# Resident feedforward weights: split in the cross attention before it, or tile by tile in the first batch that uses them

## The chip, the cores and the metric

One core of a Trainium2 chip runs the whole program. The metric is the device time of one execution in microseconds (us). TensorE does the matrix products, VectorE and ScalarE the elementwise work, GpSimd some elementwise work, and SyncE (SP) issues most of the transfers.

## What is computed

Six layers in a row over 2048 tokens of 512 features (8 batches of 256): a quantised attention, a cross attention, a feedforward with experts, an attention, a long convolution and a ternary feedforward. Each adds to its input and is followed by a layer norm. The change touches the second and the third:

```python
scores = einsum('bsd,bmd->bsm', x, ctx) / sqrt(512)          # cross attention
attn = softmax(where(mask, scores, -1e30)); out = einsum('bsm,bmd->bsd', attn, ctx)

gate_base, up_base = xf @ Wg.T, xf @ Wu.T                    # feedforward, DFF = 1408
base_out = silu(gate_base) * up_base @ Wd.T
topw, topi = top_k(softmax(xf @ Wr.T), 2)                    # 2 of 8 experts, rank 16
h = silu(gate_base + 2 * xf @ Ag.T @ Bg.T) * (up_base + 2 * xf @ Au.T @ Bu.T)
out = base_out + sum(we * 2 * h @ Ad.T @ Bd.T)
```

## The kernel before

Every layer is a stage of its own, with a barrier between stages. In a stage each engine has a list of work written out by hand; engines wait for each other on semaphores and run their lists strictly in order.

Large products are done with each operand split in two: a high part (the value copied to the rounded type fp32r, by ScalarE or VectorE) and a low part (the value minus its high part). A product is three matmuls: high by high, low by high, high by low.

**Cross attention** (`cross_attention`, L766) goes over 16 tiles of 128 tokens, two to a batch. In a step s TensorE turns tile s (L899), makes the scores of tile s-1 (L908), the output of tile s-3 (L917) and turns the probabilities of tile s-2 (L926). ScalarE copies what was turned (L938, L952) and takes the exponential (L945); VectorE masks the scores (L987 to L990), adds the output to x (L1001) and normalises. SP loads x and the context of a batch into one of three slots (L846 to L850); batch b waits until both tiles of batch b-3 are added (`added`).

In the same steps the stage prepares the feedforward's resident weights, in tiles that outlive it (`keep["experts"]`). They come as 20 pieces: AgT and AuT, AdT in two parts, WgT and WuT in halves of each of their four row blocks, of 256 to 384 KB, through five slots of `c_raw`. SP issues five pieces behind the loads of three batches, later ones as slots become free (`w_low`). ScalarE makes the high part (L957, after its copies of the step) and VectorE the low part (L1017, last in the step), one or two pieces a step.

**The feedforward** (`expert_feedforward`, L1024) has 8 batches of FT = 11 tiles of 128 hidden features; a step t is such a tile (NS = 88). `base(t)` is 24 matmuls, xhi and xlo by wg and wu (L1201). `expand` adds an expert's low rank part on top (L1214), choice 1 one step and choice 2 two steps later. `down` multiplies by ad (L1227) and wd (L1238). TensorE's order in a step t is: expand(t-2, 2), expand(t-1, 1), base(t), then some preparation of the next batch (turn x, logits, turn masks, `low_rank`, a "misc" item each, in one shared PSUM bank that the reader frees with `misc_read`), and down(t-1). Before the loop stand the preparation of batch 0 and base(0) to base(2).

ScalarE's order in a step is: the silu of choices 2 and 1 (L1335), items of the preparation, the silu of choice 0, the high part of the hidden values (L1381), and `weights_high(t+1)`: wait for entry t+1, high part of wd (L1343) and of bg (L1347). In step 5 `powers` takes an exponential (L1308), which costs a change of ScalarE's table and another back. VectorE's order is: `hidden_low` and `down_low` of the step before, the hidden values of choices 2 and 1 (L1463), `expand_low(t)` (L1482), parts of the routing (steps 4 to 8), and the hidden values of choice 0.

Streamed weights come in **entries**: entry e is Bg and Bu of tile e and WdT of tile e-1 (L1108 to L1110), in two slots. SP may issue entry e when entry e-2 is split (`entry_split`, raised by expand_low(e-2)). x comes in three slots of `xt`, loaded by ScalarE's queue (L1285).

Of the kernel before, what the change touches and what calls it, by code (L numbers as in the profile page):

```python
# [22 lines left out]
P = 128  # L23
# [742 lines left out]
def cross_attention(nc, io, sem, keep):  # L766

    NT = N // P
    XT, CT, RAW, HALF = 6, 3, 5, DFF // 2
    CUT = ((0, 6), (6, FT))
    ER = E_ * R_
    BLOCKED = 1e30
    held = ExitStack()
    fix = Maker(nc, held)
    keep["experts"] = own = dict(
        held=held, wg=[fix.sb(f"f_wg{h}", [P, KT, DFF], F32R) for h in range(2)],
        wu=[fix.sb(f"f_wu{h}", [P, KT, DFF], F32R) for h in range(2)],  # L780
        wa=[fix.sb(f"f_wa{h}", [P, 2, KT, ER], F32R) for h in range(2)],
        ad=[fix.sb(f"f_ad{h}", [P, FT, ER], F32R) for h in range(2)],
        bd=fix.sb("f_bd", [P, D]), wr=fix.sb("f_wr", [P, KT, E_]))

    PIECES = ([("a", w, 0) for w in range(2)] + [("t", 0, c) for c in range(2)] + [("g", k, c) for k in range(KT) for c in range(2)]
              + [("u", k, c) for k in range(KT) for c in range(2)])
    NP = len(PIECES)

    def pieces_of(s):

        return [n for n in range(NP) if n * NT // NP == s]

    with ExitStack() as ctx:
# [17 lines left out]
        raw = mk.sb("c_raw", [P, RAW, 6 * P])  # L811
# [4 lines left out]
        names = ("got_mask", "got_small", "mask_made", "mask_steps", "xf_done", "xf_ready", "sc_done", "score_steps", "max_ready",  # L816
                 "exp_done", "pt_done", "pt_ready", "out_done", "added", "steps", "var_ready", "root_ready", "x_ready",
                 "w_high", "w_low")
# [3 lines left out]
        piece_in = [sem(f"c_piece_in{u}") for u in range(RAW)]  # L822

        def staged(n):

            kind, a, c = PIECES[n]
            wide = {"a": KT * ER, "t": P * (CUT[c][1] - CUT[c][0])}.get(kind, HALF)
            return raw[:, n % RAW, 0:wide]

        def parts(n):  # L830

            kind, a, c = PIECES[n]
            if kind in "gu":
                return [own["w" + kind][h][:, a, c * HALF:(c + 1) * HALF] for h in range(2)]
            if kind == "a":
                return [own["wa"][h][:, a, :, :].rearrange("p k e -> p (k e)") for h in range(2)]
            return [own["ad"][h][:, CUT[c][0]:CUT[c][1], :].rearrange("p f e -> p (f e)") for h in range(2)]

        with nc.Block() as block:
            @block.sync  # L840
            def _(sp):
# [11 lines left out]
                def load_piece(n):  # L853
                    kind, a, c = PIECES[n]
                    if n >= RAW:
                        sp.wait_ge(s_["w_low"], n - RAW + 1)
                    dst = staged(n)
                    if kind in "gu":
                        src = io["WgT" if kind == "g" else "WuT"][a * P:(a + 1) * P, c * HALF:(c + 1) * HALF]
                    elif kind == "a":  # L860
                        src, dst = io["AuT" if a else "AgT"].rearrange("(k p) e -> p k e", p=P), dst.rearrange("p (k e) -> p k e", e=ER)
                    else:
                        src = io["AdT"].rearrange("(f p) e -> p f e", p=P)[:, CUT[c][0]:CUT[c][1], :]
                        dst = dst.rearrange("p (f e) -> p f e", e=ER)
                    sp.dma_start(dst, src).then_inc(piece_in[n % RAW], 16)

# [3 lines left out]
                load_x(2)  # L870
                for n in range(RAW):
                    load_piece(n)
                sp.dma_start(own["bd"][:, :], io["Bd"]).then_inc(s_["got_small"], 16)
                sp.dma_start(own["wr"][:, :, :], io["WrT"].rearrange("(k p) e -> p k e", p=P)).then_inc(s_["got_small"], 16)
# [56 lines left out]
            def _(act):  # L931
                for s in range(NT + 6):
# [33 lines left out]
            def _(dve):  # L966
# [12 lines left out]
                for s in range(NT + 5):  # L979
# [44 lines left out]
def expert_feedforward(nc, io, sem, keep):  # L1024

# [28 lines left out]
    own = keep["experts"]  # L1054
    wg, wu, wa, ad, bd, wr = (own[n] for n in ("wg", "wu", "wa", "ad", "bd", "wr"))
    with own["held"], ExitStack() as ctx:
        mk = Maker(nc, ctx)
        entry = mk.sb("f_entry", [P, 2, 2 * P + D])
# [24 lines left out]
        raw_x = raw[:, :].rearrange("p (k t) -> p k t", k=KT)  # L1083
        raw_masks = raw[:, :].rearrange("p (q j e) -> p q j e", q=TB, j=4)
# [5 lines left out]
                 "pout_read", "one_read", "two_read", "tw_steps", "tw_ready", "z_done", "bg_high", "bg_ready", "wd_high", "wd_ready", "entry_split", "tail_steps", "var_ready", "root_ready",  # L1090
                 "x_ready")
        s_ = {n: sem(f"f_{n}") for n in names}
        gu_done = [sem(f"f_gu_done_{n}") for n in CHOICES]
        got_entry = [sem(f"f_got_entry{u}") for u in range(2)]
# [6 lines left out]
        with nc.Block() as block:  # L1101
            @block.sync
            def _(sp):
                for e in range(NS + 1):
# [5 lines left out]
                    sp.dma_start(entry[:, e % 2, 2 * P:], io["WdT"][n * P:(n + 1) * P, :]).then_inc(got_entry[e % 2], 16)  # L1110
# [28 lines left out]
            def _(pe):  # L1139
# [12 lines left out]
                def logits(b):  # L1152
                    claim("lgT", b)
                    pe.wait_ge(s_["raw_ready"], (b + 1) * TB)
                    for k in range(KT):
                        last = pe.matmul(misc[0:E_, 0:T], wr[:, k, :], raw_x[:, k, :], start=(k == 0), stop=(k == KT - 1))
# [17 lines left out]
                def low_rank(b):  # L1174
                    claim("low", b)
                    pe.wait_ge(s_["lo_ready"], b + 1)
                    for w in range(2):
# [13 lines left out]
                def base(n):  # L1191
                    b, f = n // FT, n % FT
                    if f == 0:
                        pe.wait_ge(s_["lo_ready"], b + 1)
                    if n >= 3:
# [1471 lines left out]
```

## Time and profile before

| | us |
|---|---|
| median of 3 runs | 2445.17 (2442.45 to 2447.16) |
| the profiled execution | 2443.69 |
| its span in the profile | 2441.9 |
| cross attention, first issue of SP to last normalised tile | 648.2 to 769.9 |
| feedforward, first issue of SP | 773.0 |
| busy over the span: TensorE | 1885.2 (77%) |
| busy over the span: VectorE | 1536.7 (63%) |
| busy over the span: ScalarE | 900.1 (37%) |
| DMA, mean | 82 GB/s |

The numbers are shares of a program of six stages that have different limits; what a change in one of them is worth is read in that stage. In the profile times count from the start of the span. A row's bracket tells how long the engine had been idle before it, and what released it.

### The profile page before, as it was taken

Reading aid. Unit: us, or ns where it says so; the run is one execution under the profiler, and the core shown is the slowest. Engines: PE = TensorE matmul, PEld = TensorE weight load, DVE = VectorE, ACT = ScalarE, POOL = GpSimd, SP = SyncE. Lnnn points to the kernel's source line nnn. Section 1 sums busy time; section 2 is a strip of 40 time slices with the busy share of each in tenths; the row PEclk is TensorE's granted clock in tenths of the full one; section 3 lists DMA queues with packets and bytes.
Section 4 is the critical chain, followed back from the end, with each engine's and each line's share of the span. In section 5 each row is a group of like instructions: output and inputs, shape, how many; then the busy total and the mean of one; then the engine's idle time right before and its main releaser. Section 6 shows DMA issues by size and latency. Waiting matters only on the chain. (4 is left out here: it accounts for less than half of the span.)

```text
span 2441.9 us, 34261 instructions
## 1 busy us (share of the span) xinstructions
PE 1885.2 (77%) x12688; PEld 1451.1 (59%) x12688; DVE 1536.7 (63%) x3007; ACT 900.1 (37%) x1525; POOL 476.0 (19%) x478
## 2 busy tenths in 40 slices
PE   3248888614376899999999959999959997178885
PEld 2225555413254799999999948877747775034442
DVE  8747776296475556665666645565635777357876
ACT  1005555500031444444444432222222002567774
POOL 0023232000001000100010001101004766024442
PEclk9859999856587999999999979999978998588897
DMA  5099999212463112222222131100032113601000
GB/s 189 0 147 142 151 150 153 81 48 77 166 207 109 52 54 75 62 68 70 77 66 71 53 107 43 36 18 27 10 107 88 44 44 132 247 0 35 27 22 22
DMA packets 149823, 199.95 MB, mean 82 GB/s; under 512 B 13472, under 2 KB 92192, under 8 KB 147232
## 3 DMA queue, kind: packets, MB, share of 16 engines
q1 hardware_dynamic: 138400, 176.84, 28.8%
q10 hardware_dynamic: 11264, 20.98, 2.3%
q8 instruction: 101, 1.65, 0.3%
q14 instruction: 58, 0.48, 0.1%
HBM read 151.37 MB, written 46.14 MB: 81 GB/s over the span
## 5 line engine op out<-in xcount | busy, mean ns | idle before, releaser
L453 DVE TENSOR_REDUCE a_rowmax<-a_ring 128x2 f32<-128x512 f32 x256 | 165.1, 688 | 99.8 <-PE a_ring L532 97.6
L1463 DVE TENSOR_TENSOR f_hid<-f_gate,f_gu 128x256 f32<-128x256 f32 x264 | 108.5, 420 | 163.6 <-ACT f_gate L1335 161.1
L1335 ACT ACTIVATE f_gate<-f_gu 128x256 f32<-128x256 f32 x264 | 98.7, 383 | 275.3 <-PE f_gu L1201 187.2
L2185 PE MATMUL e_py<-e_kv,e_toep 128*128 128x320 f32 x640 | 180.2, 437 | 0.0
L405 ACT ACTIVATE a_prob<-a_sT 128x1024 f32<-128x1024 f32 x128 | 130.6, 1026 | 80.2 <-PE a_sT L521 80.1
L2185 PEld LDWEIGHTS e_py<-e_kv,e_toep 128*128 128x128 f32 x640 | 119.9, 191 | 46.2 <-issue 0.8
L1214 PE MATMUL f_gu<-f_lowh,f_bg 128*128 128x256 f32 x704 | 141.2, 283 | 5.3 <-POOL f_lowl L1120 5.0
L1201 PE MATMUL f_gu<-f_xhi,f_wg 128*128 128x256 f32 x704 | 130.3, 282 | 0.0
L1201 PE MATMUL f_gu<-f_xhi,f_wu 128*128 128x256 f32 x704 | 129.1, 281 | 0.0
L1214 PEld LDWEIGHTS f_gu<-f_lowh,f_bg 128*128 128x128 f32 x704 | 115.6, 191 | 9.7 <-POOL f_lowl L1120 5.2
L1468 DVE TENSOR_TENSOR f_hl<-f_hid,f_hh 128x768 fp32r<-128x768 f32 (+2 forms) x90 | 84.5, 939 | 55.9 <-ACT f_hh L1381 54.8
L1238 PE MATMUL f_pout<-f_wd,f_hh 128*128 128x512 f32 x352 | 111.5, 398 | 0.0
L1201 PEld LDWEIGHTS f_gu<-f_xhi,f_wg 128*128 128x128 f32 x704 | 108.8, 189 | 0.9 <-POOL f_xlo L1116 0.9
L1201 PEld LDWEIGHTS f_gu<-f_xhi,f_wu 128*128 128x128 f32 x704 | 107.8, 188 | 0.0
L1723 PE MATMUL d_ring<-d_xh,d_w 128*128 128x256 f32 x512 | 95.4, 288 | 12.8 <-DVE d_xl L1987 12.8
L2464 PE MATMUL g_p<-g_b,g_diag 128*128 128x512 f32 x128 | 78.3, 768 | 34.3 <-ACT g_ha L2404 34.3
L1214 PE MATMUL f_gu<-f_lowl,f_bg 128*128 128x256 f32 x352 | 99.5, 283 | 0.0
L366 POOL TENSOR_TENSOR a_y<-a_y,cb 128x512 f32<-128x512 f32 x48 | 50.0, 1043 | 253.2 <-DVE a_y L435 253.2
L1201 PE MATMUL f_gu<-f_xlo,f_wg 128*128 128x256 f32 x352 | 99.3, 282 | 0.0
L1201 PE MATMUL f_gu<-f_xlo,f_wu 128*128 128x256 f32 x352 | 99.0, 281 | 0.0
L532 PE MATMUL a_ring<-a_ks,a_qs 48*128 48x256 f32 x512 | 63.9, 328 | 45.2 <-DMA a_ks<-parts 24.8
L1381 ACT ACTIVATE f_hh<-f_hid 128x768 fp32r<-128x768 f32 (+2 forms) x90 | 74.9, 832 | 61.9 <-DVE f_hid L1463 60.2
(366 smaller groups left out, 4991.3 us busy)
## 6 DMA issues: line engine op xcount, KB each, us to landing
f_entry<-in_WdT SPq DMA_DIRECT2D x89, 256.0 KB, 2.8
a_qs<-parts SPq DMA_DIRECT2D x96, 128.0 KB, 6.4
a_ks<-parts SPq DMA_DIRECT2D x96, 128.0 KB, 7.0
parts<-a_hi SPq DMA_DIRECT2D x16, 512.0 KB, 8.7
parts<-a_lo SPq DMA_DIRECT2D x16, 512.0 KB, 9.1
e_toep<-in_taps SPq DMA_DIRECT2D x32, 256.0 KB
f_entry<-in_Bg SPq DMA_DIRECT2D x89, 64.0 KB, 1.9
f_entry<-in_Bu SPq DMA_DIRECT2D x89, 64.0 KB, 2.0
```

The source lines that it names most:

```text
L405: act.activation(prob[:, n % 4, :, :, :], sT[n % 2][:, :, :, :], ACT.Exp).then_inc(exp_done, 1)
L453: dve.tensor_reduce(rowmax[:, s % 2, :, e * SLOTS + j], ring[n % RING][:, :].rearrange("p (q t) -> p q t", t=T), AX.X, ALU.max, negate=Tru ...
L1201: last = pe.matmul(gu[n % 3][:, w, :], ws[hw][:, k, f * P:(f + 1) * P], xs[:, b % 2, k, :], start=(m == 0 and w == 0), stop=(m == 3 * KT - ...
L1214: last = pe.matmul(gu[n % 3][:, w, :], bg[:, n % BR, h, w, :], xs[:, u, j - 1, w, :], start=False, stop=True, skip_group_check=True)
L1238: last = pe.matmul(pout[q][:, :], xs[:, t % 2, 0, cols], wd[:, n % WR, h, :], start=(f == 0 and m == 0), stop=(f == FT - 1 and m == 2))
L1335: act.activation(gate[:, i % 2, :], gu[n % 3][:, 0, :], ACT.Silu).then_inc(s_["gate_ready"], 1)
L1381: act.activation(hh[:, t % 2, lo:hi, :], hid[:, lo:hi, :], ACT.Copy).then_inc(s_["hh_ready"], 1)
L1463: dve.tensor_tensor(hid[:, j, :], gate[:, i % 2, :], gu[n % 3][:, 1, :], ALU.mult).then_inc(s_["hid_ready"], 1)
L1468: dve.tensor_tensor(hl[:, t % 2, lo:hi, :], hid[:, lo:hi, :], hh[:, t % 2, lo:hi, :], ALU.subtract).then_inc(s_["hl_ready"], 1)
L1723: last = pe.matmul(dst[:, f * T:(f + 1) * T], w[hw][:, wi, k, o * P:(o + 1) * P], xs[:, k, :], start=(m == 0), stop=(m == 3 * KT - 1))
L2185: last = pe.matmul(py[n % RING][:, 0:DIAG * BS], toep[:, h % 3, (t - j) * P:(t - j + 1) * P], kv[:, h % 2, j, :], start=(j == 0), stop=(j ...
L2464: pe.matmul(p1[:, n * 512:(n + 1) * 512], diag[:, t % 2, :], b1[:, n * 512:(n + 1) * 512], start=True, stop=False)
```

## The change

The cross attention loses the pieces: no `c_raw`, no piece loads on SP, no copies on ScalarE, no subtractions on VectorE. The feedforward makes the resident tiles itself, in its first batch:

- Wg and Wu come per hidden tile as pieces of 256 KB (128 columns, so rows of 512 bytes); with AgT and AuT these are 24 pieces. Three slots hold them: the two halves of x slot 2 and `tw`, which the first batch doesn't need yet. Piece m is issued when piece m-3 is split (`w_split`).
- Pieces 0 to 7 are handled before the loop, between the items of batch 0's preparation. In the loop ScalarE makes the high parts of pieces 2s+6 and 2s+7 at the end of steps 1 to 8, after weights_high, and VectorE the low parts of pieces 2s+4 and 2s+5 in steps 2 to 9, after expand_low.
- AdT comes tile by tile in the entries (a fourth transfer, in all entries), and is split in weights_high and expand_low for e < 11.
- base(t) of batch 0 waits for its two pieces; low_rank(0) for the first two; the first logits for wr and bd. x of batch 2 is loaded at the end of step 10, no longer at the start.
- On SP entry e stands behind pieces 2e+4 and 2e+5 while e < 10.

```diff
@@ cross_attention @@
-                for s in range(NT):
-                    if s % 2 == 0 and CT <= s // 2 + 1 < B:
-                        load_x(s // 2 + 1)
-                    for n in pieces_of(s):
-                        if n + RAW < NP:
-                            load_piece(n + RAW)
-                sp.wait_ge(s_["got_small"], 32)
+                for b in range(2, B):
+                    load_x(b)
...
-                    if s < NT:
-                        for n in pieces_of(s):
-                            act.wait_ge(piece_in[n % RAW], 16 * (n // RAW + 1))
-                            act.activation(parts(n)[0], staged(n), ACT.Copy).then_inc(s_["w_high"], 1)
...
-                    if s < NT:
-                        for n in pieces_of(s):
-                            dve.wait_ge(s_["w_high"], n + 1)
-                            dve.tensor_tensor(parts(n)[1], staged(n), parts(n)[0], ALU.subtract).then_inc(s_["w_low"], 1)
@@ expert_feedforward, sync @@
+                def load_piece(m):
+
+                    if m >= 3:
+                        sp.wait_ge(s_["w_split"], m - 2)
+                    f, w = m // 2 - 1, m % 2
+                    src, cols = (("AgT", "AuT")[w], slice(0, ER)) if m < 2 else (("WgT", "WuT")[w], slice(f * P, (f + 1) * P))
+                    sp.dma_start(staged[m % 3], io[src].rearrange("(k p) o -> p k o", p=P)[:, :, cols]).then_inc(piece_in[m % 3], 16)
...
+                    sp.dma_start(entry[:, e % 2, 2 * P:3 * P], io["AdT"][f * P:(f + 1) * P, :]).then_inc(got_entry[e % 2], 16)
+
+                for m in range(3):
+                    load_piece(m)
+                sp.dma_start(wr[:, :, :], io["WrT"].rearrange("(k p) e -> p k e", p=P)).then_inc(s_["got_small"], 16)
+                sp.dma_start(bd[:, :], io["Bd"]).then_inc(s_["got_small"], 16)
+                load_entry(0)
+                load_piece(3)
+                load_piece(4)
+                load_entry(1)
+                for m in range(5, 8):
+                    load_piece(m)
+                for e in range(2, NS + 1):
+                    if e + 1 < FT:
+                        load_piece(2 * e + 4)
+                        load_piece(2 * e + 5)
+                    load_entry(e)
@@ tensor @@
+                    if b == 0:
+                        pe.wait_ge(s_["w_split"], 2 * f + 4)
@@ scalar @@
+                    if e < FT:
+                        act.activation(ad[0][:, e, :], entry[:, e % 2, 2 * P:3 * P], ACT.Copy).then_inc(s_["ad_high"], 1)
...
-                for b in range(XT):
+                def piece_high(m):
+                    f, w = m // 2 - 1, m % 2
+                    act.wait_ge(piece_in[m % 3], 16 * (m // 3 + 1))
+                    dst = wa[0][:, w, :, :] if m < 2 else (wg, wu)[w][0][:, :, f * P:(f + 1) * P]
+                    act.activation(dst, staged[m % 3], ACT.Copy).then_inc(s_["w_high"], 1)
+
+                for b in range(2):
                     load_x(b)
-                weights_high(0)
                 x_raw(0, 0)
                 x_raw(0, 1)
+                piece_high(0)
+                piece_high(1)
+                piece_high(2)
+                piece_high(3)
                 fetch_logits(0)
+                piece_high(4)
                 powers(0)
+                piece_high(5)
+                weights_high(0)
+                piece_high(6)
+                piece_high(7)
...
                     if t < NS:
                         weights_high(t + 1)
+                    if b == 0 and 1 <= s and s + 2 < FT:
+                        piece_high(2 * s + 6)
+                        piece_high(2 * s + 7)
+                    if t == FT - 1:
+                        load_x(2)
@@ vector @@
+                def piece_low(m):
+                    f, w = m // 2 - 1, m % 2
+                    dve.wait_ge(s_["w_high"], m + 1)
+                    parts = [x[:, w, :, :] for x in wa] if m < 2 else [x[:, :, f * P:(f + 1) * P] for x in (wg, wu)[w]]
+                    dve.tensor_tensor(parts[1], staged[m % 3], parts[0], ALU.subtract).then_inc(s_["w_split"], 1)
...
                 x_high(0)
+                for m in range(4):
+                    piece_low(m)
                 route_start(0)
+                piece_low(4)
+                piece_low(5)
                 route_normal(0)
                 route_choose(0)
                 route_choose(1)
                 route_weigh()
                 grow(0)
+                piece_low(6)
+                piece_low(7)
                 low_product(0)
...
                     if t < NS:
                         expand_low(t)
+                    if b == 0 and s + 1 < FT and s >= 2:
+                        piece_low(2 * s + 4)
+                        piece_low(2 * s + 5)
```

## Rows read from the trace of the kernel before

**Rows 1.** Busy us (x instructions) by engine, PEclk, DMA: feedforward, batch 1.

```profile
868.00:949.00 81.00, 81.00 (x596) 75.31 (x595) 49.84 (x114) 36.60 (x77) 7.17 (x4) 1.00 0.21 61
```

**Rows 2.** Timeline (start us, us, engine, line, what), rounds of loads in the cross attention.

```profile
689.76 1.11 PE L899 MATMUL c_pxf<-ident,c_xt 128*128 128x128 f32 x4 [4.50 <-DMA c_cf<-in_ctxFM]
...
696.22 0.38 SPq L846 DMA_DIRECT2D c_xt<-x  x1
...
703.09 1.11 PE L899 MATMUL c_pxf<-ident,c_xt 128*128 128x128 f32 x4 [3.44 <-DMA c_cf<-in_ctxFM]
...
704.00 3.10 PE L908 MATMUL c_psc<-c_cf,c_xf 128*128 128x256 f32 x8
...
709.31 1.89 PE L908 MATMUL c_psc<-c_cf,c_xf 128*128 128x256 f32 x8
...
744.34 1.12 PE L899 MATMUL c_pxf<-ident,c_xt 128*128 128x128 f32 x4 [3.64 <-DMA c_cf<-in_ctxFM]
```

**Rows 3.** Timeline, start of the cross attention.

```profile
661.00 0.66 PE L899 MATMUL c_pxf<-ident,c_xt 128*128 128x128 f32 x4 [1.38 <-DMA c_cf<-in_ctxFM]
...
666.14 0.63 ACT L957 ACTIVATE f_wa<-c_raw 128x512 fp32r<-128x512 f32 x1 [9.54 <-DMA c_raw<-in_AgT]
...
667.05 0.63 ACT L957 ACTIVATE f_wa<-c_raw 128x512 fp32r<-128x512 f32 x1 [0.28 <-DMA c_raw<-in_AuT]
...
668.22 3.78 PE L908 MATMUL c_psc<-c_cf,c_xf 128*128 128x256 f32 x8 [6.56 <-ACT c_xf L938]
...
683.18 0.38 SPq L846 DMA_DIRECT2D c_xt<-x  x1
```

**Rows 4.** Timeline, end of the cross attention.

```profile
756.98 0.89 DVE L1017 TENSOR_TENSOR f_wu<-c_raw,f_wu 128x704 fp32r<-128x704 f32 x1
```

**Rows 5.** Timeline, feedforward before its loop.

```profile
777.56 1.12 PE L1149 MATMUL f_misc<-ident,f_xt 128*128 128x128 f32 x4 [11.46 <-DMA f_xt<-x]
...
780.92 0.42 ACT L1347 ACTIVATE f_bg<-f_entry 128x256 fp32r<-128x256 f32 x1 [17.16 <-DMA f_entry<-in_WdT]
...
787.31 0.80 PE L1201 MATMUL f_gu<-f_xhi,f_wg 128*128 128x256 f32 x2
...
791.46 0.17 DVE L1414 COPY f_route<-f_misc 128x16 f32<-128x16 f32 x1 [7.00 <-PE f_misc L1163]
...
795.98 1.17 DVE L1446 TENSOR_SCALAR f_raw<-f_route 128x128 f32<-128x128 f32 x8
...
800.17 0.50 PE L1181 MATMUL f_misc<-f_xhi,f_wa 128*128 128x256 f32 x2 [0.79 <-ACTq L1322]
```

**Rows 6.** Groups by line in the cross attention: busy us, mean ns, idle before.

```profile
L1017 DVE TENSOR_TENSOR f_wa<-c_raw,f_wa 128x512 fp32r<-128x512 f32 x2 | 1.4, 692 | 9.3 <-ACT f_wa L957 9.3
```

**Rows 7.** WdT's transfers (L1110): ns of issue, min/median/max; landing.

```profile
L1110 SPq DMA_DIRECT2D f_entry<-in_WdT x89: 333/432/1485, 773.8 to 1416.7; - x89
...
DMA to landing us min/median/max: 2.6/2.8/7.0
```

**Rows 8.** Timeline, steps 3 to 9 of the feedforward's first batch.

```profile
818.46 0.39 ACT L1335 ACTIVATE f_gate<-f_gu 128x256 f32<-128x256 f32 x1 [0.54 <-PE f_gu L1214]
...
832.04 0.62 ACT L1343 ACTIVATE f_wd<-f_entry 128x512 fp32r<-128x512 f32 x1
832.56 0.40 ACT L1347 ACTIVATE f_bg<-f_entry 128x256 fp32r<-128x256 f32 x1
...
841.63 1.28 ACT L1335 ACT_TABLE_LOAD   x1
842.92 0.66 ACT L1335 ACTIVATE f_gate<-f_gu 128x256 f32<-128x256 f32 x2
...
844.09 0.42 DVE L1482 TENSOR_TENSOR f_bg<-f_entry,f_bg 128x256 fp32r<-128x256 f32 x1
...
861.45 0.39 PE L1201 MATMUL f_gu<-f_xhi,f_wg 128*128 128x256 f32 x2
...
864.29 0.40 PE L1181 MATMUL f_misc<-f_xhi,f_wa 128*128 128x256 f32 x2
```

More of the change, by code:

```diff
@@ L771, in cross_attention @@
     NT = N // P
-    XT, CT, RAW, HALF = 6, 3, 5, DFF // 2
-    CUT = ((0, 6), (6, FT))
-    ER = E_ * R_
+    XT, CT = 6, 3
     BLOCKED = 1e30
[L776 to L791, printed above, removed]
     with ExitStack() as ctx:
@@ L815, in cross_attention @@
         pout = [mk.ps(f"c_pout{i}", [P, 512]) for i in range(2)]
-        names = ("got_mask", "got_small", "mask_made", "mask_steps", "xf_done", "xf_ready", "sc_done", "score_steps", "max_ready",
-                 "exp_done", "pt_done", "pt_ready", "out_done", "added", "steps", "var_ready", "root_ready", "x_ready",
-                 "w_high", "w_low")
+        names = ("got_mask", "mask_made", "mask_steps", "xf_done", "xf_ready", "sc_done", "score_steps", "max_ready",
+                 "exp_done", "pt_done", "pt_ready", "out_done", "added", "steps", "var_ready", "root_ready", "x_ready")
         s_ = {n: sem(f"c_{n}") for n in names}
@@ L851, in load_x @@
                                  ).then_inc(got_x[b % CT], 16)
[L853 to L865, printed above, removed]
                 load_x(0)
@@ L1052, in group @@
         return js[0], js[-1] + 1, INDEX[t, js[0]]
-    own = keep["experts"]
-    wg, wu, wa, ad, bd, wr = (own[n] for n in ("wg", "wu", "wa", "ad", "bd", "wr"))
-    with own["held"], ExitStack() as ctx:
+    with ExitStack() as ctx:
         mk = Maker(nc, ctx)
-        entry = mk.sb("f_entry", [P, 2, 2 * P + D])
+        wg = [mk.sb(f"f_wg{h}", [P, KT, DFF], F32R) for h in range(2)]
+        wu = [mk.sb(f"f_wu{h}", [P, KT, DFF], F32R) for h in range(2)]
+        wa = [mk.sb(f"f_wa{h}", [P, 2, KT, ER], F32R) for h in range(2)]
+        ad = [mk.sb(f"f_ad{h}", [P, FT, ER], F32R) for h in range(2)]
+        bd = mk.sb("f_bd", [P, D])
+        wr = mk.sb("f_wr", [P, KT, E_])
+        entry = mk.sb("f_entry", [P, 2, 3 * P + D])
         wd = mk.sb("f_wd", [P, WR, 2, D], F32R)
@@ L1083, in expert_feedforward @@
         raw_x = raw[:, :].rearrange("p (k t) -> p k t", k=KT)
+        staged = [xt[:, 2, q, :].rearrange("p (k c) -> p k c", k=KT) for q in range(TB)]
+        staged.append(tw[:, :, :].rearrange("p j t -> p (j t)").rearrange("p (k c) -> p k c", k=KT))
         raw_masks = raw[:, :].rearrange("p (q j e) -> p q j e", q=TB, j=4)
@@ L1093, in expert_feedforward @@
         gu_done = [sem(f"f_gu_done_{n}") for n in CHOICES]
+        piece_in = [sem(f"f_piece_in{u}") for u in range(3)]
         got_entry = [sem(f"f_got_entry{u}") for u in range(2)]
@@ L1103, in _, with load_entry @@
             def _(sp):
[L1104 removed]
+                def load_piece(m):
[4 more added lines that the diff above has]
+                    sp.dma_start(staged[m % 3], io[src].rearrange("(k p) o -> p k o", p=P)[:, :, cols]).then_inc(piece_in[m % 3], 16)
+                def load_entry(e):
                     if e >= 2:
@@ L1342, in weights_high @@
                             act.wait_ge(s_["taken"], n - WR + 1)
-                        act.activation(wd[:, n % WR, 0, :], entry[:, e % 2, 2 * P:], ACT.Copy).then_inc(s_["wd_high"], 1)
+                        act.activation(wd[:, n % WR, 0, :], entry[:, e % 2, 3 * P:], ACT.Copy).then_inc(s_["wd_high"], 1)
+                    if e < FT:
+                        act.activation(ad[0][:, e, :], entry[:, e % 2, 2 * P:3 * P], ACT.Copy).then_inc(s_["ad_high"], 1)
                     if e < NS:
@@ L1473, in down_low @@
                     dve.wait_ge(s_["wd_high"], n + 1)
-                    last = dve.tensor_tensor(wd[:, n % WR, 1, :], entry[:, (n + 1) % 2, 2 * P:], wd[:, n % WR, 0, :], ALU.subtract)
+                    last = dve.tensor_tensor(wd[:, n % WR, 1, :], entry[:, (n + 1) % 2, 3 * P:], wd[:, n % WR, 0, :], ALU.subtract)
                     last.then_inc(s_["wd_ready"], 1)
@@ L1481, in expand_low @@
                     dve.wait_ge(s_["bg_high"], e + 1)
+                    if e < FT:
+                        dve.wait_ge(s_["ad_high"], e + 1)
+                        dve.tensor_tensor(ad[1][:, e, :], entry[:, e % 2, 2 * P:3 * P], ad[0][:, e, :], ALU.subtract)
                     dve.tensor_tensor(bg[:, e % BR, 1, :, :], entry[:, e % 2, 0:2 * P].rearrange("p (w c) -> p w c", w=2),
```

32 lines of the change are left out of this document (11 added, 21 removed).

## The prediction

> **What bounds the kernel now.** I read the page first, then the mean of each stretch, then the timeline of the two stages that the change touches, and last the single operations that move. In the feedforward TensorE is the bound: over batch 1 it is busy 81.00 of 81 us at a granted clock of 1.00, while VectorE is busy 49.8 and ScalarE 36.6 [rows 1]. Whatever holds TensorE up there is paid in full; work on the other engines is free only as long as nothing that TensorE waits for stands behind it. The cross attention has no such bound. Its steady state is a closed circle over three context slots: when the second tile of a batch is added, SP issues the load of the batch three further on (696.22), TensorE sits idle until that has landed (703.09), computes, and releases the next load [rows 2]. Four such rounds take 689.76 to 744.34, 13.65 us each. So its splitting is mostly hidden in the middle and costs at the two ends.
>
> **The change part by part.** The sum is made on the profiled execution, span 2441.9 us, 2443.69 in all; the median of the three runs is 2445.17, 1.5 us more, so I add the sum to the median.
>
> *Cross attention, start: 8.4 us less.* ScalarE stands idle for 9.54 us in front of the first piece, until 666.14, because the AgT piece is queued behind three batches of loads; the copy of the turned tile 1 stands behind it, so the scores of tile 1 start at 668.22, though TensorE had turned tile 2 at 661.00 [rows 3]. Without pieces the scores of tile 1 follow that turn, at 662.0. They run at half clock and take 3.0 (as the 3.10 of the eight after a gap, against 1.89 of the eight at 709.31 [rows 2]), to 665.0. Then turn 0.6 and scores 1.9 of tile 2, the output of tile 0 (waits for its probabilities, 667.5 to 669.4), turn 0.6, scores 1.9, output 1.9 of the next tiles, and the add of tile 1 0.75: the load of batch 3 goes out at 674.8 and not at 683.18. Batch 2 (lands by 665.2, since the piece behind it lands at 666.14) is in time.
>
> *Middle: 2.7 us less.* From issue to TensorE's turn the loads take 6.58 us for batch 3 (683.18 to 689.76) and 6.87 for batch 4 [rows 2, 3]; the later ones share the queues with pieces. Undisturbed I take 6.5, and the computing part of the round, 6.45, stays: 12.95 a round against 13.65, four rounds. Bounds: 0 (pieces disturb nothing) and 4 (6.3 a load). The split copies and subtractions themselves win nothing here, VectorE and ScalarE wait for TensorE.
>
> *End: 1.5 us less.* In the last tiles nothing is loaded and VectorE is behind; two subtractions of 0.89 [rows 4] lie on the way to the last scores. Bounds 0 and 2.5. The stage gains 12.6 in all, bounds 9 and 15.
>
> *Feedforward, before its loop: 6.9 us more.* ScalarE no longer stands before the first entry (780.92 [rows 5]) but copies the turned x when the turn at 777.56 is over, about 778.8, so xhi and xlo are there some 2 us earlier. That is eaten: base(0) needs pieces 0 to 3, and piece 3 is issued only once piece 0 is subtracted (three slots). Copy of piece 0 to 781.7, its subtraction to 782.7 (0.63 and 0.69 each [rows 3, 6]), landing 2.9 later (2.8 is the median of WdT's, also 256 KB [rows 7]), copy, subtraction: 787.2, the 787.31 of before. The x loads and small loads are 2.5 MB against 2.3, hence 0 to 1.3 for this term; 0 taken. Then the order on VectorE counts: subtraction 4 stands behind route_start, which comes after base(0) (791.46), and subtraction 5 behind the copy that follows powers: 793.9, so base(1) starts 2.6 late. Subtractions 6 and 7 stand behind the whole routing, whose grow (795.98 to 797.15) ends 1.45 later than before, and then take 1.4: base(2) starts at 800.0 and, with the 2.84 that a base takes (861.45 to 864.29 [rows 8]), ends at 802.9. Before, it ended as grow did, at 797.1, and the mask turns followed: 5.8 late. The two gaps of 2.5 to 3 us drop the clock: the eight score matmuls show 1.2 us for one such gap [rows 2]. I take 1.1 for both together, bounds 0 and 2.4. low_rank(0), at 800.17 before, comes at 807.1.
>
> *Feedforward, steps 2 to 8: 18.8 us more.* This is the term that decides. Per step come one ad copy (about 0.25), one ad subtraction and two pieces on each engine, about 1.5 us each; these would fit beside TensorE. The queue does not. SP's list is piece 2e+4, piece 2e+5, entry e. Piece 2e+5 waits until subtraction 2e+2 is done, and VectorE does that one in step e-1, in the middle; entry e is needed by weights_high(e) in that same step e-1. Before, entry e went out a whole step earlier. So a circle closes outside TensorE. From T, the end of the first subtraction of a step: issue of the piece 0.45, of Bg and Bu 0.9 (0.43 is the median issue [rows 7]), WdT's landing 2.8 after its issue [rows 7], AdT just behind it 0.25: T + 4.4. ScalarE then splits wd (0.62), ad, bg (0.40) and two pieces (0.63 each), which overlap by 0.1 each as the starts 832.04 and 832.56 show [rows 8]: 2.1. Only then comes the silu of choice 2 of the next step; from its start to the start of expand_low's subtraction the trace has 842.92 to 844.09, and with its 0.42, a completion wait of 0.14, the ad and one piece 0.69 it is 2.6 to the next T [rows 6, 8]. With 0.2 of semaphores: 9.3 us a step. TensorE's step is 7.4 in batch 1 (81 us for eleven); without the tail work of a batch before it I take 7.1. Laid on the clock of before (the 6.9 counted apart): in step 2 T is 817.4, the entry lands at 821.8, silu of step 3 starts at 823.95, not at 818.46 [rows 8]. Five rounds of 9.3, and 2.8 more in step 5, where the exponential and two table loads of 1.28 are in the same circle [rows 8], bring the silu of step 8 to 873.2, the next T to 875.8, the entry to 880.25, the copies to 882.35, the masks' copies to 883.1. low_rank(1) waits for these; before it started at 864.29 [rows 8]. Bounds: a round of 8.8 or 9.9, so 16 to 22. After step 9 the entries lead again, and nothing is won back since TensorE is the bound.
>
> *At nothing.* AdT is loaded with all 89 entries; from step 9 on that 0.3 us lies in a load that leads by a step. The load of x(2) at step 10 waits for piece 23, long done, and is needed in step 12; if it were late, it costs at most its landing of 4.5 [rows 5]. take_one's new wait stands after step 11 and holds up nothing.
>
> *Where a page and the trace differ.* Pieces have rows of 512 bytes. In the trace AuT, 256 KB in such rows, lands 0.9 us after AgT in a full queue [rows 3], so I price a piece as an entry's WdT. The Trainium skill, "DMA: Bandwidth & Descriptors", section Bandwidth, asks for 1 MiB a transfer and gives 0.95 us for 64 KB and 6.15 us for 1 MB; in between, an estimate from that page, 256 KB would take 2.0 us, 1.1 more than here. By it a round would be some 1.1 longer and the sum about 6 us higher, 2464.
>
> The sum: -12.6 + 6.9 + 18.8 = +13.1, so 2445.2 + 13.1 = 2458.3.
>
> **The rivals.**
> (a) *The circle does not bind.* Then only the start of the feedforward is paid: -12.6 + 6.9 = -5.7, 2439.5, faster. Place: weights_high(3) to weights_high(9). It decides at a landing within 2.2 us of T, which would bring the round to TensorE's 7.1. For it: ScalarE is busy only 36.6 of 81 us [rows 1]. Against: the fastest landing of WdT is 2.6 [rows 7], with three issues ahead of it. Chance 0.07.
> (b) *Part of it is covered*, because T comes earlier in a step than I have it or the entry lands sooner (round of 8.0): the steps cost about 11, and the sum is +5, 2450; below that the difference is lost in the measurement. For it: TensorE's own steps 1 and 2 are short, and 4 to 8 differ. Chance 0.15.
> (c) *TensorE becomes slower than the circle.* Each round leaves it 2.2 us idle, and after such gaps it runs at half clock (3.10 for 1.89 [rows 2]). A step of 7.1 with 3 us at half clock is 8.6, still within 9.3. If it stayed at half clock for longer, 6 us, it would be 10.1, 0.8 over the circle, 7 steps: +6, 2464; at half clock throughout 14.2, +34. Chance 0.13.
> (d) *The cross attention gains little*: the first loads, not ScalarE, set its pace, and the circle of loads keeps it. Gain 4 in place of 12.6, 2467. Against: the idle of 9.54 in front of the first piece [rows 3]. Chance 0.08.
>
> **How the numbers follow.** Forecast 0.57 for 2452 to 2464 around 2458. The bounds of the terms, taken together, give 2447 to 2468; towards (c) and (d) I go to 2470, towards (b) to 2446. A difference of about 0.2%, 4.9 us, is what a measurement of this kernel tells from none. Faster by more than that: 0.07, from (a). Within: 0.13, most of (b) and the edge of the gain. Slower: 0.80.
>
> **What would show it.** The profile after should have the first c_xf copies at 656 and 657; rounds of about 13 us; a cross attention some 12.6 shorter; base(1) and base(2) after gaps of 2.5 and 3 us with VectorE's piece subtraction as releaser; ScalarE's f_wd copies in steps 2 to 8 waiting about 1 to 2 us for the entry's DMA, SP's entry issues standing behind a piece, TensorE below full busy until about 883 + 7 - 13 = 877, and 81 us a batch afterwards. Wrong it is if the silu of steps 3 to 8 come 7 to 8 us apart, or if TensorE's matmuls in these steps run at half clock for most of the time.

## The result and the profile after

The changed kernel takes 2465.74 us (median of 4 runs, 2461.59 to 2468.98), the kernel before, run beside it, 2446.16 (4 runs, 2442.45 to 2453.64): ratio 1.007, 95% interval 1.0054 to 1.0086. It is slower, by 0.7% as the ratio is estimated from all the runs and by 19.6 us between the two medians. The profiled execution of the changed kernel took 2461.59 us (span 2459.7), that of the kernel before 2443.69 (span 2441.9), so the traces show 17.8 us of it. The prediction was 2458, with 2446 to 2470 as its range.

Three marks cut the stretch of the change: SP's first issue of the feedforward (ends the cross attention's stage, whose own first issue is at 648.15 before and 648.66 after), the first low_rank product, and the second one.

| us | before | after | difference | predicted |
|---|---|---|---|---|
| cross attention, first issue to the feedforward's first issue | 124.83 | 111.60 | -13.2 | -12.6 |
| feedforward's first issue to low_rank(0) | 27.19 | 33.83 | +6.6 | +6.9 |
| low_rank(0) to low_rank(1): steps 0 to 9 | 64.12 | 87.23 | +23.1 | +18.8 |
| began later +0.5, behind the last mark +0.8 | | | +1.3 | |

One trace is one execution. The cross attention has the same code in the changed kernel and in experiments 1 to 5 below, and in their six traces it took 110.6 to 113.6 us; so the first row is known to some 2 us. The steps in the changed kernel's order took 87.2, 89.6 and 88.0 (changed kernel, experiments 3 and 4).

Busy times of the changed kernel by stretch; the columns are those of [rows 1]: stretch, length, then busy us and instructions of PE, PEld, DVE, ACT and POOL, the granted clock, DMA share and GB/s.

```profile
760.26:774.90 14.64, 5.39 (x16) 2.35 (x17) 5.60 (x13) 3.76 (x7) 2.72 (x1) 0.60 0.65 198
774.90:794.10 19.20, 13.95 (x85) 13.07 (x85) 7.13 (x32) 4.34 (x11) 0.00 (x0) 0.82 0.36 104
794.10:870.00 75.90, 57.41 (x357) 50.25 (x357) 39.79 (x96) 35.40 (x76) 4.75 (x2) 0.87 0.30 88
953.00:1034.00 81.00, 80.95 (x600) 75.35 (x599) 51.21 (x118) 36.92 (x79) 7.17 (x4) 1.00 0.27 77
```

The third row is most of the loss: from low_rank(0) to the end of ScalarE's step 7 TensorE is busy 57.4 of 75.9 us, VectorE 39.8 and ScalarE 35.4, so a chain across engines holds it up and not the work of one. The fourth is batch 1: 80.95 of 81 us at full clock, as in [rows 1]: in batch 1 nothing changed.

The cross attention, timeline (start us, us, engine, line, what); these answer to [rows 2, 3]:

```profile
661.53 0.66 PE L836 MATMUL c_pxf<-ident,c_xt 128*128 128x128 f32 x4 [1.15 <-DMA c_cf<-in_ctxFM]
...
673.41 0.37 SPq L807 DMA_DIRECT2D c_xt<-x  x1
...
680.13 1.12 PE L836 MATMUL c_pxf<-ident,c_xt 128*128 128x128 f32 x4 [3.48 <-DMA c_cf<-in_ctxFM]
...
686.65 0.37 SPq L807 DMA_DIRECT2D c_xt<-x  x1
...
727.56 0.37 SPq L807 DMA_DIRECT2D c_xt<-x  x1
```

The load of batch 3 goes out at 673.41, against 683.18. The four rounds behind it take (727.56 - 673.41) / 4 = 13.54 us each. The load still needs 6.7 us from issue to TensorE's turn (673.41 to 680.13). In the kernel before the last load went out here:

```profile
737.26 0.38 SPq L846 DMA_DIRECT2D c_xt<-x  x1
```

The start of the feedforward answers to [rows 5]:

```profile
769.77 3.44 DVE L1524 TENSOR_TENSOR f_wa<-f_xt,f_wa 128x512 fp32r<-128x512 f32 x2
769.94 2.72 POOL L1079 TENSOR_TENSOR f_xlo<-f_raw,f_xhi 128x1024 fp32r<-128x1024 f32 x1 [13.35 <-DVE f_xhi L1402]
...
774.93 0.48 PE L1170 MATMUL f_gu<-f_xhi,f_wg 128*128 128x256 f32 x2 [2.36 <-DVE f_wu L1524]
...
782.36 0.80 PE L1170 MATMUL f_gu<-f_xhi,f_wg 128*128 128x256 f32 x2 [2.29 <-DVE f_wu L1524]
...
788.30 0.50 PE L1170 MATMUL f_gu<-f_xhi,f_wg 128*128 128x256 f32 x2 [1.34 <-DVE f_wu L1524]
...
794.09 0.51 PE L1148 MATMUL f_misc<-f_xhi,f_wa 128*128 128x256 f32 x2 [0.79 <-ACTq L1293]
```

base(0), base(1) and base(2) each start behind a gap, and the one named as releaser is VectorE's subtraction of a piece (L1524).

One round of the steps, from one subtraction of a Wg piece to the next:

```profile
829.81 0.69 DVE L1524 TENSOR_TENSOR f_wg<-f_xt,f_wg 128x512 fp32r<-128x512 f32 x1
...
830.53 0.38 SPq L1048 DMA_DIRECT2D f_xt<-in_WuT  x1
830.96 0.50 SPq L1054 DMA_DIRECT2D f_entry<-in_Bg  x1
...
831.98 0.43 SPq L1056 DMA_DIRECT2D f_entry<-in_WdT  x1
832.45 0.43 SPq L1057 DMA_DIRECT2D f_entry<-in_AdT  x1
...
835.46 0.63 ACT L1314 ACTIVATE f_wd<-f_entry 128x512 fp32r<-128x512 f32 x1 [2.54 <-DMA f_entry<-in_AdT]
...
836.50 0.62 ACT L1327 ACTIVATE f_wg<-f_tw 128x512 fp32r<-128x512 f32 x1
837.02 0.62 ACT L1327 ACTIVATE f_wu<-f_xt 128x512 fp32r<-128x512 f32 x1
837.54 0.64 ACT L1306 ACTIVATE f_gate<-f_gu 128x256 f32<-128x256 f32 x2
...
839.45 0.69 DVE L1524 TENSOR_TENSOR f_wg<-f_tw,f_wg 128x512 fp32r<-128x512 f32 x1
...
840.17 0.38 SPq L1048 DMA_DIRECT2D f_tw<-in_WuT  x1
```

Read it as a circle. The subtraction frees a slot, SP may issue the WuT piece at 830.53, and only behind it in SP's list stand the entry's four transfers. ScalarE stands idle for 2.54 us for the last of them, then splits the entry and two pieces, and only then runs the silu on which VectorE and TensorE wait; the next subtraction lets the next WuT piece go 9.64 us later. The waits of the third stretch above (who waited for what: us in total, times, longest) name the same two links, 14.7 us of ScalarE for the entry and 8.4 us of TensorE for what follows the silu (a seventh wait for the entry, 4.25 us in step 8, comes behind the stretch):

```profile
ACT f_wd L1314 <- DMA f_entry<-in_AdT: 14.7, 6, 3.2
...
PE f_gu L1183 <- DVE f_hid L1455: 8.4, 4, 3.2
```

### The profile page after: what moved, and what is told of

The parts are those of the page before. It is cut to its first block and busy times, and to the rows that moved or that the text cites. A ratio compares the mean times of both kernels' runs of the same rounds, so it can differ in the third digit from the quotient of the medians.

```text
span 2459.7 us, 34389 instructions
## 1 busy us (share of the span) xinstructions
PE 1894.9 (77%) x12672; PEld 1459.4 (59%) x12688; DVE 1541.0 (63%) x3022; ACT 902.6 (37%) x1540; POOL 476.4 (19%) x478
```

## The experiments

The theory under test: the steps are slow because the entry stands behind a piece in SP's list. Rival theories: the added splitting itself is too much for ScalarE and VectorE, or TensorE's clock is what is lost. For the start of the feedforward: the order in which copies and subtractions stand in ScalarE's and VectorE's programs, against the arrival of the pieces.

**1. The entry ahead of the pieces in SP's list.**

```
                 for e in range(2, NS + 1):
+                    load_entry(e)
                     if e + 1 < FT:
                         load_piece(2 * e + 4)
                         load_piece(2 * e + 5)
-                    load_entry(e)
```

> The changed kernel, with one move on SP: entry e is issued ahead of pieces 2e+4 and 2e+5, not behind them. Theory A (the circle T, entry's transfer, weights_high, silu, next T): the entry leads by a step again, the rounds of 9.7 us in steps 2 to 8 fall to TensorE's 7.1 to 7.6, ScalarE no longer waits for AdT before the f_wd copies; from low_rank(0) to low_rank(1) 66 to 68 us (64.1 in the kernel before, 87.2 in the changed one); the whole within 3 us of the kernel before, 2443 to 2449. Theory B (the additional copies and subtractions themselves fill ScalarE and VectorE, whatever the queue does): rounds stay at 9 or more, the whole at 2458 or more. Theory C (TensorE's lower clock in the gaps costs the time): rounds stay at 9 while TensorE's matmuls are 0.41 us long.

Measured: 2446.57 (10 runs) against 2447.57 of before (16 runs) beside it, ratio 1.000 (0.9988 to 1.0012). By moving one line of SP's program the whole loss of the change is gone. low_rank(0) to low_rank(1) falls from 87.23 to 69.56 (66 to 68 expected), while every copy and subtraction is still there; the start of the feedforward stays (33.65). Stretch from low_rank(0) to low_rank(1), then ScalarE's copy of the entry in step 5, which waits for no DMA any more:

```profile
795.30:865.00 69.70, 59.86 (x411) 54.81 (x412) 45.38 (x109) 40.52 (x90) 4.76 (x2) 0.93 0.41 121
```

```profile
835.07 0.61 ACT L1314 ACTIVATE f_wd<-f_entry 128x512 fp32r<-128x512 f32 x1
```

So 17.7 of the 23.1 us are SP's order. The other 5.4 are left with the splitting in the steps. 2.9 of them are in one wait of TensorE for the hidden product, 3.2 where the kernel before has 0.3. It is the step of the exponential, and both engines are later there. On ScalarE the copies of the ad tile and of two pieces stand ahead of the two table loads: from the high part of the hidden values to the first silu behind the loads it is 5.76 (834.31 to 840.07), 4.51 before. On VectorE the ad subtraction and two pieces stand ahead of the routing: from the hidden values of choice 2 to those of choice 0 it is 4.49 (840.56 to 845.05), 3.09 before. Another 1.9 is TensorE's own work: the same matmuls keep it busy for 59.7 us between the two marks and not 57.9, at a granted clock of 0.93 and not 0.95.

```profile
PE f_gu L1183 <- DVE f_hid L1455: 3.2, 1, 3.2
```

**2. The pieces ahead of the entry in ScalarE's program**, SP's list as in the changed kernel. If the circle is the cause, a round must shrink by what ScalarE does in the circle between landing and silu.

```
-                    if t < NS:
-                        weights_high(t + 1)
                     if b == 0 and 1 <= s and s + 2 < FT:
                         piece_high(2 * s + 6)
                         piece_high(2 * s + 7)
+                    if t < NS:
+                        weights_high(t + 1)
```

> The changed kernel, with ScalarE's two piece copies of a step ahead of weights_high, not behind it. Theory A: they are then made while the entry is still on its way, and come out of the circle: 1.05 us less a round, 8.65 instead of 9.7, seven rounds, 6 to 7 us less than the changed kernel, 2458 to 2460. Theory B (ScalarE's load itself): no difference, within 2 us of the changed kernel, 2464 to 2468. Theory C: no difference either, since TensorE's gaps stay.

Measured: 2454.77 (5 runs), ratio 1.0039 (1.0024 to 1.0053), 11 us under the changed kernel's 2465.74 and below the 2458 to 2460 expected. The entry's copies start 9.3, 8.7 and 8.6 us apart (812.65, 821.96, 830.64, 839.25), still waiting for AdT, and low_rank(0) to low_rank(1) is 80.62, 6.6 less. That is the part that belongs to the edit; 3.3 more of the trace's 10.1 lie in and ahead of the cross attention, where the two kernels are the same. The same work in another order shortened the circle by about the two copies, so the circle set the pace and not the amount of work. It is a partial repair: SP's order is worth 17.7 in the trace, this 6.6.

**3. The order before the loop.** ScalarE copies pieces 5 and 6 ahead of powers(0), no longer behind it, and VectorE subtracts pieces 4 and 5 ahead of the routing and 6 and 7 between its parts, not behind it.

```
                 fetch_logits(0)
                 piece_high(4)
-                powers(0)
                 piece_high(5)
-                weights_high(0)
                 piece_high(6)
+                powers(0)
                 piece_high(7)
+                weights_high(0)
...
-                for m in range(4):
+                for m in range(6):
                     piece_low(m)
                 route_start(0)
-                piece_low(4)
-                piece_low(5)
+                piece_low(6)
                 route_normal(0)
+                piece_low(7)
                 route_choose(0)
...
                 grow(0)
-                piece_low(6)
-                piece_low(7)
```

> The changed kernel, with the pieces ahead of the routing before the loop: VectorE's subtractions 4 and 5 before route_start, 6 behind it and 7 behind route_normal; ScalarE's copies 5 and 6 before powers. Theory: base(1) and base(2) follow base(0) without the gaps of 2.3 and 1.3 us, and the mask turns wait for grow alone: low_rank(0) 29.3 us after the stage's first issue instead of 33.8 (27.2 in the kernel before), the whole 4.5 us below the changed kernel, 2461. Rival (the gaps are covered by something later, since the loop begins with waits for lowl): less than 1 us.

Measured: 2465.33 (5 runs), ratio 1.0059 (1.0038 to 1.0081): no gain that can be told, where 4.5 were expected. low_rank(0) comes 32.04 after the first issue, 1.8 earlier, and in this trace, the slowest of the five runs, the steps behind it take 89.64, 2.4 more. Piece 5 held up the start (timeline):

```profile
779.23 1.10 SPq L1048 DMA_DIRECT2D f_tw<-in_WuT  x1
...
784.38 0.63 ACT L1327 ACTIVATE f_wu<-f_tw 128x512 fp32r<-128x512 f32 x1 [4.00 <-DMA f_tw<-in_WuT]
```

SP issued it behind entry 1, whose four issues take about 0.45 each, its own issue took 1.10, and it was there 5.15 after the issue. The same mistake of order as in the steps: a transfer that is wanted stands behind one that isn't.

**4. The same, with SP's entry 1 behind pieces 3 to 7.**

```
                 load_entry(0)
-                load_piece(3)
-                load_piece(4)
-                load_entry(1)
-                for m in range(5, 8):
+                for m in range(3, 8):
                     load_piece(m)
+                load_entry(1)
```

> The kernel with pieces ahead of the routing (start order alone, where piece 5 was issued 2.4 us behind piece 4 because entry 1 stood between them, and landed only at 784.4, 5.2 us after its issue), with entry 1 behind piece 7. Theory: piece 5 lands 3 us after its issue, the gap of 2.8 us ahead of base(1) closes, low_rank(0) 1.5 to 3 us earlier than there (32.0 after the first issue): 29 to 30.5; the whole 2 to 3 us lower, 2462. Rival (the ring of three slots and not entry 1 holds piece 5): low_rank(0) within 0.5 us of 32.0. The rounds in the loop stay at 9.7.

Measured: 2461.59 (5 runs), ratio 1.0053 (1.0035 to 1.007). Piece 5 goes out at 777.67, 0.60 behind piece 4 and not 2.40, and its copy starts at 780.77, 16.8 after the stage's first issue and not 20.5. low_rank(0) comes at 29.33, 4.5 earlier than in the changed kernel and 2.7 earlier than in experiment 3, as expected. The whole doesn't show it safely: the intervals of the two ratios overlap, and in the trace the steps take 88.00 (0.8 more) and the unchanged cross attention 113.6 (2.0 more), so that its span, 2460.2, is no shorter than the changed kernel's 2459.7. What is shown is the time to low_rank(0).

**5. All orders together**: experiments 1 and 4, and pieces 0 and 1 copied between the two halves of x and subtracted ahead of x's split.

```
                 x_raw(0, 0)
-                x_raw(0, 1)
                 piece_high(0)
                 piece_high(1)
+                x_raw(0, 1)
...
+                piece_low(0)
+                piece_low(1)
                 x_high(0)
-                for m in range(4):
+                for m in range(2, 6):
                     piece_low(m)
```

> The changed kernel with three orders changed: entry e ahead of pieces 2e+4 and 2e+5 on SP; before the loop entry 1 behind piece 7 and the pieces ahead of the routing; and pieces 0 and 1 copied between the two x copies and subtracted ahead of x_high, so that VectorE doesn't subtract them while GpSimd makes xlo (where the first two took 3.44 us, not 1.3). Theory (circle and order of the start explain the whole loss): low_rank(0) 29 us after the stage's first issue (33.8 changed, 27.2 before), 69.5 us on to low_rank(1), so 4 to 5 us below the kernel with entry first alone, 2440 to 2443 beside 2446 to 2447 of before. Rival (the time before the loop is bound by the transfers of seven pieces at 3 us each, in a ring of three): low_rank(0) at 32 or more, the whole at 2445 or more.

Measured: 2441.82 (12 runs) against 2447.40 (24 runs), ratio 0.9978 (0.9968 to 0.9989). low_rank(0) comes at 26.47, 0.7 earlier than in the kernel before; the steps take 71.70. Expected were 29 and 69.5, so the forecast of the whole, 2440 to 2443, was met by two misses that cancel. The steps are 2.1 longer than in experiment 1 because the same matmuls keep TensorE busy for 62.0 us and not 59.7, at a granted clock of 0.88 and not 0.93. With the same work and the same slots the change is now a gain of 0.2% on the kernel before. Against experiment 1 it is 4.8 us in the medians, and the two intervals just touch. The first rows of its feedforward:

```profile
767.72 1.29 DVE L1522 TENSOR_TENSOR f_wa<-f_xt,f_wa 128x512 fp32r<-128x512 f32 x2 [7.55 <-ACT f_wa L1325]
...
773.11 0.47 PE L1168 MATMUL f_gu<-f_xhi,f_wg 128*128 128x256 f32 x2 [0.59 <-DVE f_wu L1522]
```

The two subtractions that took 3.44 us beside GpSimd take 1.29 ahead of GpSimd's, and the gap in front of base(0) is 0.59, not 2.36.

**6. No pieces at all**: the kernel before without the loads, copies and subtractions of Wg, Wu, Ag, Au and Ad. Left out of the computation is exactly that; the resident tiles are filled with zeros by GpSimd.

> The kernel before, without the loading and splitting of Wg, Wu, Ag, Au and Ad in the cross attention: this part is left out, the resident tiles are filled with zeros by GpSimd meanwhile. Theory A's ledger: the cross attention (first issue of SP to the feedforward's first issue, 124.8 us before, 111.6 in the changed kernel) takes 111.6 here too and the feedforward is unchanged, so 13 us less than before, 2433. Rival (the changed kernel's shorter cross attention has another cause, or zeros from GpSimd disturb it): between 2436 and 2446. The rounds of loads should stay at 13.5 us, so all of it at the two ends, about 10 at the start and 3 at the end.

Measured: 2430.04 (5 runs), ratio 0.9938 (0.9918 to 0.9958), 17.5 us less; the interval allows 10 to 20. In the profile of the slowest but one of the five (2436.57) the cross attention is 9.2 shorter, where 13.2 were expected, and the feedforward's part about as before (26.70 and 64.44). The difference is at the start: the load of batch 3 goes out at 28.75 after the first issue, 24.75 in the changed kernel. The fills show as most of the reason. VectorE's first mask copy, 0.29 us in the kernel before, takes 6.18 beside them and ends 0.15 after the fills of the second row; the first tile's scores, made at 662.2, are masked from 665.45 on and not before:

```profile
658.50 6.18 DVE L969 CAST c_mask<-c_mask 128x256 f32<-128x256 uint8 x1 [12.13 <-DMA c_mask<-in_mask]
659.61 4.92 POOL L889 MEMSET f_wu<- 128x1408 f32 x4
```

With the 4.0 us of the start given back the stage would be 13.2 shorter, an estimate from the two traces, and that is what the changed kernel shows. The end of the stage, from the last load's issue on, is 32.4, against 35.7 before and 32.7 changed. The rounds of loads without any piece (SP's issues, timeline; the fills run beside the first three):

```profile
678.66 0.37 SPq L846 DMA_DIRECT2D c_xt<-x  x1
...
733.11 0.37 SPq L846 DMA_DIRECT2D c_xt<-x  x1
```

Four rounds in 54.45, 13.61 each, against 13.52 with pieces: in the middle they cost nothing that can be seen.

**7. The kernel before, with its first piece in step 3.** If the gain in the cross attention is its start, it must be had there without touching the feedforward.

```
-        return [n for n in range(NP) if n * NT // NP == s]
+        return [n for n in range(NP) if n * (NT - 3) // NP == s - 3]
```

> The kernel before, with the 20 pieces handled in steps 3 to 15 of the cross attention, not 0 to 15; all work is done. Theory (the first pieces' transfers, for which ScalarE and VectorE stand in steps 0 and 1, make the start slow): the load of batch 3 goes out 25 to 27 us after the stage's first issue instead of 35.0, the rounds stay at 13.5 to 14, the whole 7 to 9 us below the kernel before, 2438 to 2440. Rival (the transfers or the splitting work themselves, wherever they stand, cost the time): less than 3 us won.

Measured: 2439.83 (10 runs), ratio 0.9972 (0.9958 to 0.9986), 7.6 us less in the medians, 5.4 in the trace. The load of batch 3 goes out at 26.92 after the stage's first issue (35.03 before), 8.1 earlier; four rounds, now with the pieces in fewer steps, take 14.3 each (674.72, 689.29, 703.38, 717.86), which gives part of it back, and the stage is 120.68, 4.2 shorter. The rounds were expected to stay at 13.5 to 14. The feedforward is untouched (26.16, 1.0 less in this trace, and 64.20). So the start is shown as the place of the loss, 8.1 us of it, but with all 20 pieces still in the stage about half of that was kept. This and experiment 5 both beat the two kernels; between them the intervals overlap.

## Why the prediction was right, and where its terms were off

The sum was +13.1; the traces show +17.8 and the medians +19.6. Of the 7.4 us between 2458.3 and 2465.7, 4.7 are terms of the sum, 1.8 lie between traces and medians, and the kernel before was itself 1.0 higher in the runs beside it. The place and the mechanism of the loss were right; its largest term was too small.

*Cross attention, start: -8.4 predicted, -10.3 measured* (35.03 to 24.75 after the first issue). The mechanism was the one named: ScalarE no longer stood for 9.54 us in front of the first piece [rows 3]. Experiment 7 has it alone, 8.1.

*Middle: -2.7 predicted, none measured.* This step failed: there was nothing to win. I took 6.5 for a load in undisturbed queues and 12.95 for the round, against 13.65. But 13.65 was the spacing of TensorE's turns [rows 2]; from issue to issue the rounds of before were 13.52 (683.18 to 737.26, four rounds). After the change they are 13.54, without any piece 13.61, and 13.1 to 14.1 in the six traces that have this code; none comes down to 12.95. The premise was wrong: the pieces did not slow the loads, which took 7.1 from issue to turn in the mean of five before and 7.0 after. Its bound of 0 was the value.

*End: -1.5 predicted, -3.0 measured*, from the last load's issue to the feedforward's first (35.72 to 32.70). That is 0.5 outside its bound. The stage came out as forecast, -13.2 for -12.6, since too little at both ends and too much in the middle cancelled; that nearness is luck.

*Feedforward before its loop: +6.9 predicted, +6.6 measured.* base(0) starts 14.67 after the first issue and started at 14.33; base(1) and base(2) start behind gaps of 2.29 and 1.34 with VectorE as releaser, as foretold, the second smaller than its 3. Experiments 4 and 5 show by how much the order made it: 4.5 with the subtractions and entry 1 moved, 2.9 more with pieces 0 and 1 ahead of x's split, and the whole term is gone.

*Steps 2 to 8: +18.8 predicted, +23.1 measured.* The circle is the one described, and experiments 1 and 2 show it from both sides. What was off is its size. T is, as in the prediction, the end of the first piece subtraction of a step. In the order of the forecast: the first T comes 17.0 after low_rank(0), forecast 17.2. The six rounds behind it (WuT's issues at 811.09, 820.81, 830.53, 840.17, 852.80, 862.64, 872.47) take 61.4 us, forecast 58.6 (five of 9.3 and one of 12.1). And from the last T to low_rank(1) it is 8.9, forecast 7.3. Together 4.2 of the 4.3 us by which the term fell short. Both misses are the same sub-step, the landing of the entry. I had it at T + 4.4, with AdT 0.25 behind WdT. In the round above T is 830.50 and the copy starts at 835.46, T + 4.96 (5.0 to 5.2 in the six rounds): AdT's issue alone is 0.47 behind WdT's, and it lands 3.0 after it, for its median of 2.5. At the last T, with the next entry's four issues right behind, it is T + 6.1:

```profile
872.47 0.38 SPq L1048 DMA_DIRECT2D f_tw<-in_WuT  x1
...
874.38 0.43 SPq L1057 DMA_DIRECT2D f_entry<-in_AdT  x1
874.86 1.80 SPq L1054 DMA_DIRECT2D f_entry<-in_Bg  x1
...
878.50 0.63 ACT L1314 ACTIVATE f_wd<-f_entry 128x512 fp32r<-128x512 f32 x1 [4.25 <-DMA f_entry<-in_AdT]
...
881.32 0.80 PE L1148 MATMUL f_misc<-f_xhi,f_wa 128*128 128x256 f32 x2 [3.14 <-ACTq L1293]
```

*The rivals.* (a), the circle doesn't bind, is refuted: ScalarE waits for the entry seven times, 19.0 us in all. What it describes is experiment 1, where nothing of the steps but 5.4 is left. (b), a shorter round, didn't come true. (c) was half true: the gaps did lower the granted clock, to 0.87 over the steps (the third row of the stretches above) and to 0.53 in the stretch below, and low_rank(1) begins at half of full clock (0.80 for two products, 0.40 in [rows 8]). From low_rank(0) to low_rank(1) it made TensorE busy for 64.5 us, where the same matmuls took 57.9 before. But TensorE's slower step stayed within the round, as ScalarE's wait for the entry in every round shows, and behind the last mark only 0.8 us more were lost.

```profile
850.00:860.00 10.00, 6.03 (x26) 5.73 (x27) 6.12 (x18) 4.09 (x10) 0.00 (x0) 0.53 0.35 101
```

(d), a gain of 4 in the cross attention, is refuted by the first table.

*The price of a transfer.* I set the trace's price of a 256 KB piece, some 2.8 us to its landing, against an estimate from the Trainium skill, "DMA: Bandwidth & Descriptors", section Bandwidth, which made a round 1.1 longer. (The two times that the Trainium skill gives there are those of transfers that GpSimd issues, without the time to issue them.) The transfers of the changed kernel (KB each, median us from issue to landing):

```profile
f_entry<-in_WdT SPq DMA_DIRECT2D x89, 256.0 KB, 2.7
...
f_xt<-in_WuT SPq DMA_DIRECT2D x7, 256.0 KB, 3.0
```

WuT's pieces took 3.0, those of WgT, issued behind an entry, 3.5 to 4.0; the entry's WdT, which is what the circle waits for, kept 2.7. The rounds were 0.4 longer than mine, by AdT's landing; the lengthening that the Trainium skill's figures gave was 1.1. For the round the row was the nearer price.

## What to carry to other kernels

An in-order queue of issues is a wait of its own: a transfer that stands behind one which waits for a slot waits for that slot too, and if that slot is freed by work behind the transfer's own data, a circle can close, here of 9.7 us, although the busiest engine works three quarters of the time. Before moving loads, write down for each issue when it may go and when its data is wanted, and put what is wanted first, first; here one line's place was worth 19 us between the medians, as much as the change cost. And of work that is to be moved off a stage, ask first what it really costs there: here most of it was its place in the first steps, and one changed line in the old stage gave back 7.6 us in the medians without a new home for the work.

## What the runs showed of the hardware

VectorE's subtraction and GpSimd's, both with two inputs in SBUF, hold each other up. In the changed kernel the first of the two f_wa subtractions starts at 769.77, GpSimd's at 769.94. GpSimd's takes 2.72, where it took 2.35 in the kernel before (784.54) with nothing on VectorE beside it, and the second f_wa subtraction takes 2.83 where the first takes 0.69 (the line's instructions from 769 to 800, ns min/median/max):

```profile
L1524 DVE TENSOR_TENSOR f_wa<-f_xt,f_wa x2: 685/1760/2834, 769.8 to 770.4; 128x512 fp32r<-128x512 f32 x2
```

VectorE's two took 3.44 together and 1.29 where nothing ran on GpSimd (experiment 5). Later the two engines meet again:

```profile
831.79 2.41 POOL L1079 TENSOR_TENSOR f_xlo<-f_raw,f_xhi 128x1024 fp32r<-128x1024 f32 x1 [29.71 <-DVE f_xhi L1402]
...
832.96 2.06 DVE L1460 TENSOR_TENSOR f_hl<-f_hid,f_hh 128x768 fp32r<-128x768 f32 x1 [0.91 <-ACT f_hh L1368]
```

2.06 us for an operation that takes 0.96 elsewhere. It ends at 835.02, 0.82 after GpSimd's end at 834.20. The Trainium skill, "SBUF — State Buffer", section "SBUF: two separate sides", says that a VectorE instruction with two SBUF inputs and a GpSimd instruction that reads SBUF exclude each other for the whole instruction, the later one being blocked. By that, the second f_wa subtraction would end 0.69 behind GpSimd's end (769.94 + 2.72 = 772.66), at 773.35; it ended at 773.21. By the same rule the later one would end at 834.20 + 0.96 = 835.16 and ended at 835.02. The trace agrees, to 0.14 us in both.

The time of an issue isn't fixed either: SP's issues took 0.38 to 0.50 in the round shown, 1.80 for the Bg issue above and 1.10 for piece 5 in experiment 3, behind the four transfers of an entry; in the same place of the changed kernel it took 0.43 (775.63). And the small AdT transfer, 64 KB, landed 2.5 us after its issue in the median, 4.1 at the last T, where a whole entry and not one piece was issued right behind it. Whether that is the cause was not tested.
